# Low halves of the attention weights on GpSimd in quarter pieces, and the RMS root asked earlier

## The reference, cut to what matters

```python
x = x + L0_xattn(layernorm(x), ctx)       # quantized matmul q1 @ q2
x = x + L0_ffn(layernorm(x), ...)         # RMS norm, 24 logits per token, Sinkhorn, mixing
x = x + L1_xattn(layernorm(x), ctx, ...)  # attention with Wq, Wk, biases
x = x + L1_ffn(layernorm(x), ...)         # gated FFN with low-rank terms

# L0_ffn
x_norm = x * rsqrt(mean(x * x) + RMS_EPS)
logits = x_norm @ [W_res; W_pre; W_post].T + base      # 16 + 4 + 4 per token
H_res = sinkhorn_log(H_res_logits)                     # 50 iterations of row and column normalization of a 4x4
H_pre, H_post = softmax(...), softmax(...)
y = (sum_n H_pre[n] * x_n) @ W_branch
out = H_res @ x_streams + H_post[n] * y

# L1_xattn: scores = (text Wq.T + bq)(features Wk.T + bk).T / 32
```

## Time and profile before

| what | value |
|---|---|
| median of 3 runs | 1202.49 us (1200.74 to 1203.63) |
| profiled execution, its own time | 1200.88 us |
| its span, first to last instruction | 1199.1 us |
| TensorE (PE) busy | 1141.1 us, 95% of the span |
| VectorE (DVE) busy | 793.9 us, 66% |
| ScalarE (ACT) busy | 482.3 us, 40% |
| GpSimd (POOL) busy | 149.3 us, 12% |
| mean granted TensorE clock | 0.987 |

### The profile page before, as it was taken

One profiled execution on the slowest core, in us unless ns is written; L12 is line 12 of the kernel. 1 busy time (PEld: TensorE's weight loads), 2 busy tenths in 40 slices (PEclk: granted clock), 3 DMA queues, 4 the chain that ended last, 5 costly groups with the idle time before them and its releaser, 6 DMA issues.

```text
span 1199.1 us, 16583 instructions
## 1 busy us (share of the span) xinstructions
PE 1141.1 (95%) x6452; PEld 569.9 (48%) x6458; DVE 793.9 (66%) x1589; ACT 482.3 (40%) x727; POOL 149.3 (12%) x141
## 2 busy tenths in 40 slices
PE   4877999899989999989999999999999999999998
PEld 2444454644545444554444444444444444444444
DVE  8999889888983278967766767677676552222220
ACT  6785653772253324444434343443433331111110
POOL 4762340081004010200000000000001000000000
PEclk9997999999999999999999999999999999999999
DMA  9620000132032042201121211212112221111310
GB/s 372 250 93 1 2 1 1 71 97 80 1 106 84 7 134 106 106 0 71 36 71 36 71 53 53 71 36 71 36 53 62 98 78 48 48 48 48 131 40 18
DMA packets 26062, 83.58 MB, mean 70 GB/s; under 512 B 3648, under 2 KB 4288, under 8 KB 25984
## 3 DMA queue, kind: packets, MB, share of 16 engines
q1 hardware_dynamic: 25984, 82.53, 19.9%
HBM read 76.22 MB, written 6.29 MB: 69 GB/s over the span
## 4 chain that ended last, share of the span: by engine, by line
PE 72%; DVE 20%; ACT 4%; issue 2%; DMA 1%; POOL 0%; SPq 0%; ACTq 0%; DVEq 0%
PE PAIR L2333 32%; PE PAIR L1975 11%; PE PAIR L1976 11%; PE PAIR L1977 11%; DVE X L1412 2%; DVE PAIR L1364 2%; PE PAIR L2290 1%; DVE LORA L1363 1%; DVE LORA L1365 1%; DVE BST L1214 1%; DVE BST L1215 1%; PE PAIR L2345 1%; DVE X L1285 1%; PE PAIR L2151 1%; DVE XT L1279 1%
## 5 line engine op out<-in xcount | busy, mean ns | idle before, releaser
L1975 PE MATMUL PAIR<-POOL 128*128 128x512 f16 x672 | 255.7, 381 | 2.1 <-DVE POOL L1455 2.1
L1976 PE MATMUL PAIR<-POOL 128*128 128x512 f16 x672 | 255.6, 380 | 0.0
L1977 PE MATMUL PAIR<-POOL 128*128 128x512 f16 x672 | 255.5, 380 | 0.0
L2333 PE MATMUL PAIR<-XT,POOL 128*128 128x512 f16 (+1 forms) x1056 | 239.0, 379 | 1.0 <-ACT ST L889 1.0
L2333 PEld LDWEIGHTS PAIR<-XT,POOL 128*128 128x128 f16 (+1 forms) x1056 | 102.6, 98 | 120.5 <-issue 2.5
L2333 PE MATMUL PAIR<-X,POOL 128*128 128x512 f16 (+1 forms) x528 | 121.2, 379 | 0.0
L1977 PEld LDWEIGHTS PAIR<-POOL 128*128 128x128 f16 x672 | 65.8, 98 | 80.3 <-issue 1.4
L1975 PEld LDWEIGHTS PAIR<-POOL 128*128 128x128 f16 x672 | 65.6, 98 | 67.6 <-DVE POOL L1455 3.9
L1976 PEld LDWEIGHTS PAIR<-POOL 128*128 128x128 f16 x672 | 65.7, 98 | 63.8 <-issue 0.3
L1585 DVE SCALAR_TENSOR_TENSOR STG<-STG,PAIR 128x1024 f32<-128x1024 f32 (+2 forms) x32 | 28.2, 885 | 92.4 <-PE PAIR L2345 89.1
L923 ACT ACTIVATE POOL<-STG 128x1024 f16<-128x1024 f32 (+2 forms) x32 | 25.0, 788 | 145.2 <-DVE STG L1585 145.2
(11 more groups left out here) (296 smaller groups left out, 1738.9 us busy)
## 6 DMA issues: line engine op xcount, KB each, us to landing
STG<-in_gate_w SPq DMA_DIRECT2D x21, 512.0 KB, 3.4
STG<-in_up_w SPq DMA_DIRECT2D x21, 512.0 KB, 4.2
STG<-in_ctx_t SPq DMA_DIRECT2D x16, 512.0 KB, 4.2
STG<-in_ctx SPq DMA_DIRECT2D x16, 512.0 KB, 4.3
STG<-in_down_w SPq DMA_DIRECT2D x16, 512.0 KB, 3.5
POOL<-in_ctx SPq DMA_DIRECT2D x12, 512.0 KB, 11.2
X<-in_x SPq DMA_DIRECT2D x8, 512.0 KB, 9.8
out_t<-X SPq DMA_DIRECT2D x16, 256.0 KB, 2.9
```

Source lines behind the costliest of these rows:

```text
L1975: e.matmul(dst, l_hi, r_hi, start=first, stop=False)
L1976: e.matmul(dst, l_hi, r_lo, start=False, stop=False)
L1977: return e.matmul(dst, l_lo, r_hi, start=False, stop=last)
L2333: i = e.matmul(dst, blk[:, a_, k, :], src[:, b_, k, :], start=(opens and k == 0 and n == 0), stop=(k == KD // 2 - 1 and n == 2), skip_grou ...
```

## The change

GpSimd makes the low halves of weights 0 to 14, each in four instructions of 256 columns instead of one of 1024; VectorE keeps weight 15 alone. ScalarE gives weights 13 and 14 the second pass, and runs `weight_hi(13)` and `weight_hi(14)` directly after `weight_hi(12)`, ahead of `second_transposed(6)`. The RMS root is formed from the variances (`reciprocal(VE)`) instead of from the finished layer-norm scale, so that `logits_root` no longer needs `norm_rest(4, 8)`: VectorE asks for it right after `norm_ask(4, 8)`, and ScalarE takes the two roots one after the other. The part of the logits that needs the means (`logits_mean`) moves up with it, and `bias_operands` moves from between `norm_ask(0, 4)` and `second_lo(4)` to behind it. `second_lo(7)` moves ahead of `norm_rest(4, 8)`.

```diff
-        ON_VECTOR = (13, 14, 15)
+        ON_VECTOR = 15
...
             def weight_lo(i):
                 e.wait_ge(w_hi, i + 1)
-                e.tensor_tensor(W2[i][:, 1, :], FSTAGE[i + AHEAD], W2[i][:, 0, :], ALU.subtract).then_inc(wp_lo, 1)
+                for q in range(0, D, CST):
+                    qs = slice(q, q + CST)
+                    last = e.tensor_tensor(W2[i][:, 1, qs], FSTAGE[i + AHEAD][:, qs], W2[i][:, 0, qs], ALU.subtract)
+                last.then_inc(w_lo, 1)
...
             weight_lo(12)
+            weight_lo(13)
+            weight_lo(14)
             for g in range(NT):
                 branch_sum(g)
...
             weight_hi(12)
+            weight_hi(13)
+            weight_hi(14)
             second_transposed(6)
+            take_logits(0)
             norm_root(4, 8)
-            take_logits(0)
-            weight_hi(13)
+            root(RX2, RX)
             second_transposed(7)
-            weight_hi(14)
             weight_hi(15)
-            root(RX2, RX)
             take_logits(1)
...
             def logits_root():
-                e.wait_ge(ln_ok, 2 * NT)
-                chain(e.tensor_tensor(RN, RST, RST, ALU.mult))
+
+                e.wait_ge(var_ok, 6)
+                chain(e.reciprocal(RN, VE))
                 chain(e.tensor_tensor(RN, RN, MV[:, :, 1], ALU.mult))
                 e.tensor_scalar(RX, RN, RMS_EPS, None, ALU.add).then_inc(var_ok, 1)
+
+            def logits_mean():
+
+                bc = [P, NT, NLOG]
+                e.wait_ge(wsum_ok, 1)
+                chain(e.tensor_tensor(LTMP, MV[:, :, 0].unsqueeze(2).to_broadcast(bc),
+                                      WSUM.unsqueeze(1).to_broadcast(bc), ALU.mult))
...
                 last.then_inc(soft_ok, 1)
-                weight_lo(14)
                 e.wait_ge(sink_a, 2)
...
             norm_ask(0, 4)
-            bias_operands()
             second_lo(4)
             norm_rest(0, 4)
...
             norm_ask(4, 8)
+            logits_root()
+            logits_mean()
+            bias_operands()
             second_lo(6)
+            second_lo(7)
             norm_rest(4, 8)
-            second_lo(7)
-            logits_root()
-            weight_lo(13)
             logits()
```

More of the change, by code:

```diff
@@ L281, in build @@
                              "x_clip", "q_clip"))
-        smh_ok, c2_ok, ht_lo, wp_lo = sem("smh_ok"), sem("c2_ok"), sem("ht_lo"), sem("wp_lo")
+        smh_ok, c2_ok, ht_lo, wv_lo = sem("smh_ok"), sem("c2_ok"), sem("ht_lo"), sem("wv_lo")
         ctx_ok, x1_ok, w_lo, sink_v, soft_v, soft_ok, share_ok, hr_ok, mixed, bias_ok = (
@@ L330, in build @@
             + [(("dfold", m, i), d_add, m * NP + i + 1) for m in range(KD) for i in range(NP)]))
-        ON_VECTOR = (13, 14, 15)
+        ON_VECTOR = 15
         def weight_done(e, i):
-            e.wait_ge(w_lo if i in ON_VECTOR else wp_lo, sum((n in ON_VECTOR) == (i in ON_VECTOR) for n in range(i + 1)))
+            if i < ON_VECTOR:
+                e.wait_ge(w_lo, i + 1)
+            else:
+                e.wait_ge(wv_lo, i - ON_VECTOR + 1)
         def factor_place(n):
@@ L690, in weight_hi @@
                 last = e.activation(W2[i][:, 0, :], st, ACT.Copy, scale=WS)
-                if i not in ON_VECTOR:
+                if i < ON_VECTOR:
                     last = e.activation(st, st, ACT.Copy, scale=WS)
@@ L760, in mix_help @@
                 e.wait_ge(hr_ok, 1)
-                e.wait_ge(wp_lo, 2 * KD - len(ON_VECTOR))
-                e.wait_ge(w_lo, len(ON_VECTOR))
+                weight_done(e, ON_VECTOR - 1)
+                weight_done(e, 2 * KD - 1)
                 for sj in (2, 3):
@@ L1297, in logits @@
                 chain(e.tensor_tensor(RN, RN, RST, ALU.mult))
-                e.wait_ge(wsum_ok, 1)
-                chain(e.tensor_tensor(LTMP, MV[:, :, 0].unsqueeze(2).to_broadcast(bc),
-                                      WSUM.unsqueeze(1).to_broadcast(bc), ALU.mult))
                 e.wait_ge(lg_raw, B)
@@ L1399, in weight_lo @@
                 e.scalar_tensor_tensor(W2[i][:, 1, :], FSTAGE[i + AHEAD], WS, W2[i][:, 0, :], ALU.mult,
-                                       ALU.subtract).then_inc(w_lo, 1)
+                                       ALU.subtract).then_inc(wv_lo, 1)
             def mix(g, sj0=0, sj1=None):
```

## The result

| | before | after |
|---|---|---|
| median | 1202.13 us (1200.74 to 1203.63, 4 runs) | 1195.66 us (1194.12 to 1196.99, 4 runs) |
| profiled execution, its own time | 1200.88 us | 1196.09 us |
| its span | 1199.1 us | 1194.3 us |

The ratio is 0.9941, with a 95% interval of 0.9927 to 0.9956: 7.1 us faster by the ratio, 6.5 by the medians, where 3.8 were forecast. The mechanism came as described in the main: the large links of the chain moved the right way, and two small ones didn't come as forecast (`norm_rest(4, 8)` took turns, and the clock fell again for a shorter time). The gain is nearly twice the sum. So the question for the experiments is which term was too small.

A forecast was written before the change was run, and what follows sets the result against it. TensorE, busy 1141 of 1199 us, was taken as the bound, its waits ended by VectorE's late chain. Chain 2.5 plus clock 1.3 made 3.8 us, from the median 1202.49 to 1198.7; range 1195.2 to 1202.0.

The forecast's parts named there:

- the wait for weight 15: TensorE's wait at M's eighth step, for weight 15's low half: some 2.8 us instead of 4.1.
- The clock: TensorE's granted clock behind M's step 8: 1.3 us taken of the 2.2 us expected if it stays high.
- min(y, x + 2.2): At the mixing: what a gain x on VectorE's chain and y on TensorE's M is worth, in us.
- The log wait: In sinkhorn_start: VectorE must wait for ScalarE's logarithm, so moving out weight 14's 1.13 us saves only 0.5.
- the chain's gain x: VectorE's chain to Sinkhorn gains 2.5 us: 2.1 from its tail and weight 14, 0.4 earlier in the front.
- the last one or two wait a piece: VectorE's norm_rest(0, 4) in GpSimd's gap: small delay at its end, add_product(6) at 84.3 to 84.4, 6.0 us earlier.
- nine instructions that take turns [...] at 0.69 each that is 6.2: Behind norm_ask(4, 8): small VectorE instructions alternate with GpSimd's pieces, 0.69 us each, 6.2 us together.
- this is hidden by 3.4 us: ScalarE's transposed tile 6, held back to 94.3, is still ready before VectorE's second_lo(6) at 97.7.
- `norm_rest(4, 8)` runs free: VectorE's tail to Sinkhorn: GpSimd's lows end at 99.7, so these instructions take no turns and cost 1.2 us.
- the earlier front: Near 41.52 us, small VectorE instructions cross shorter GpSimd pieces: gain between 0 and 0.8 us, 0.4 taken.
- Rival 4: GpSimd's pieces cost 0.53 us each and the clock stays high: 6.5 us gained, 1196.0 us; chance 0.10.
- Rival 3: Pieces cost GpSimd too much: chain gain used up at 0.85 us each, 1205 us at 0.95; chance 0.08.

The follow-up runs named there:

- e7: Changed kernel with weight 15's low half on GpSimd too: 1196.09 us, ratio 0.9949 to the kernel before.
- e11: Changed kernel with bias_operands moved behind the softmax in sinkhorn_start, into the wait for ScalarE's logarithm: 1197.61 us, ratio 0.9955 to the kernel before.
- e1: Kernel before with one edit, GpSimd's low halves in four pieces of 256 columns: 1195.97 us, ratio 0.9957 to the kernel before.
- e3: Changed kernel with bias_operands back between norm_ask(0, 4) and second_lo(4): 1200.04 us, ratio 0.9987 to the kernel before.
- e6: Changed kernel with pieces of 128 columns, eight to a low half: 1206.83 us, ratio 1.0037 to the kernel before.
- e4: Changed kernel with the low halves of weights 13 and 14 back on VectorE: 1196.59 us, ratio 0.9953 to the kernel before.
- e10: e3 with a reciprocal of four numbers put ahead of norm_ask(4, 8): 1200.36 us, ratio 0.9974 to the kernel before.
- e16: e3 with a tensor_tensor of four numbers put ahead of norm_ask(4, 8): one execution, 1201.16 us.
- e17: e3 unchanged, profiled a second time: one execution, 1199.64 us.
- e19: e18 with bias_operands also moved behind the softmax, as in e11: 1197.18 us, ratio 0.9957 to the kernel before.
- e5: Changed kernel with pieces of 512 columns, two to a low half: 1199.58 us, ratio 0.9973 to the kernel before.
- e2: Changed kernel with each GpSimd low half again one instruction of 1024 columns: 1199.75 us, ratio 0.9985 to the kernel before.
- e18: Changed kernel with ScalarE's transposed tiles and roots ahead of the high halves of weights 13 to 15: 1197.67 us, ratio 0.9963 to the kernel before.
- e13: Changed kernel with a reciprocal of four numbers put ahead of norm_ask(4, 8): 1197.46 us, ratio 0.9957 to the kernel before.
- e14: Changed kernel where each piece waits on a semaphore for the piece before it: 1198.80 us, ratio 0.9969 to the kernel before.

## Why the prediction was too small

Right, by its own steps: the wait for weight 15 (forecast 2.8, measured 2.77). The clock (forecast 1.3 us back): from step 8 to the mixing it was 204.56 - 111.40 = 93.16 before and is 197.95 - 105.73 = 92.22, so 0.9 came back. That term was a choice between two outcomes, and neither came whole: the clock fell again, but for 3.6 us instead of 5.8. That 0.9 lies near 1.3 is luck. The rule that ties M and VectorE's chain, min(y, x + 2.2): the chain gained 202.07 - 196.95 = 5.1 (its last instruction, `hr_ok`, starts there), M 6.6, and min(6.6, 7.3) is what the mixing gained. e7 shows the other side: with M far ahead the chain holds the mixing, at 197.79. The log wait was used up as worked out (0.52 us of it left).

The step that failed is one term of the sum, the chain's gain x: "x = 2.5". It measured 5.7 us at weight 15's low half, which starts step 8 (105.73 for 111.40), and 5.1 at the factors; in between one small copy of the Sinkhorn part (L1385, at 138.99) met a GpSimd instruction and took 0.72 us instead of 0.19. So the sum 2.5 + 1.3 = 3.8 came as 5.7 + 0.9 = 6.6 at the mixing. The error of x in its parts:

- **"the last one or two wait a piece"**, `add_product(6)` at 84.3 to 84.4: it came at 81.94. All six instructions passed in GpSimd's gap, since `norm_ask(0, 4)` was issued at 79.57, not 80.51, and took 0.17. Of these 0.94 us, 0.6 were there at 40 us already, 0.5 of them at 11 us, ahead of the first low half; the rest came from the pieces in the front. The 0.5 at 11 us is a difference between two executions (before, VectorE waits 0.56 us for ScalarE there) and not the change's. The 81.94 doesn't hang on it: in the eight profiles with this order, 256 columns and no semaphore wait between pieces, `norm_ask(0, 4)` was issued between 77.64 and 79.88 and `add_product(6)` came between 81.50 and 82.41. 2.4 us, the largest error.
- **"nine instructions that take turns [...] at 0.69 each that is 6.2"**, and 0.2: from 88.83 to 93.26 they took 4.4. Six waited (0.33, 0.60, 0.90, 0.53, 0.59, 0.52), three got in for 0.15 to 0.17, among them two of the three that don't wait for their predecessor (the third is the mean part, L1307, 0.90 us where its own length is 0.36). 2.0 us. A piece is 0.63, not 0.69. The reciprocal that is new in `logits_root` was rightly left out: it needs no turn.
- **"this is hidden by 3.4 us"**, said of ScalarE's transposed tile 6, forecast for 94.3 with VectorE there at 97.7: it was done at 93.16, when VectorE had just arrived (93.13). Had the turns cost nothing, VectorE would have waited here, as e11 shows. `bias_operands`, charged with 3.6, cost nothing.
- **"`norm_rest(4, 8)` runs free"**: it did not. Arriving at 95.57 with pieces until 97.25 it took 2.1 us instead of 1.2, two of its instructions 0.60 each. This error of 0.9 has the other sign.

Together 2.4 + 2.0 - 0.9 = 3.5, nearly the 3.6 us from the forecast 102.5 to VectorE's softmax at 98.90. The 0.4 us that the forecast added for the earlier front is contained in it, which leaves 3.2, the 5.7 less 2.5. e1 shows besides that the moved instructions gave this chain nothing: with the pieces alone it was as early. Rival 4 (cheap pieces, 1196.0) is nearest in time, but not by its mechanism: pieces cost 0.63, not 0.53. The Trainium skill's estimate of 0.56 per piece ("GPSIMD Engine Reference", section "Elementwise — side-by-side cycle accounting") was as far from 0.63 on one side as the row's 0.69 on the other. Its rule of the shared port ("Advanced Engine Details and Errata", section "Mode Summary", where it is stated of VectorE's two-port instructions) held in 195 trains, for `tensor_tensor` too, as a wait for one piece, and the eight long stalls, of up to 24 pieces, go beyond what it says.

Rival 3, slower through GpSimd, was priced for pieces of 0.8 us and more. The danger that the runs showed instead is the standing `norm_ask`: e3 kept 1.6 us of the gain with it, and e6, with two of them and the longer low halves, had a loss. The prediction had no case for it, and the profile of before shows none.

## What to carry to other kernels

Where two engines take turns at a port, the length of one instruction on the slower one is the price of every small instruction on the other; cutting it in four cost that engine 20% more time (2.55 us for 2.13) and gave this kernel 5 us. The reordering around it gave 1 to 2 more at most. Count what really takes a turn (here: not the reciprocals, `bn_aggr` or PSUM readers), place small chains in the other engine's gaps, and look in the profile after for a small instruction that stood over many pieces. When a chain gets faster, look up what was hidden behind it by less than the gain, here ScalarE's transposed tile.

## What the hardware showed that I had not expected

A VectorE instruction of four numbers stood for 3, 6, 6, 7, 8, 11 and 24 boundaries between GpSimd pieces (2.0 to 9.2 us in e4, e3, e10, e16, e17, e6 and e6; 3 again in e19), while its neighbours got in at each boundary. Seven of the eight ended within 0.03 us of the last piece; the longest, e6's second, was let go with four more pieces to come. Alone, with the same instructions, this never came in 195 trains. And the clock's cost behind TensorE's wait for weight 15 came in steps and not with the length of the wait. From step 8 to the mixing it took 90.6 us after waits of 1.3, 1.5, 2.0 and 2.0 us (e17, e10, e16, e3; there to the end of tile 6, as VectorE was later), 92.0 to 92.3 after 2.1, 2.1, 2.3, 2.8, 3.2, 3.4, 3.5 and 6.0 (e6, e5, e2, changed, e4, e11, e18, e19), 93.2 to 93.6 after 3.2, 3.9, 4.1 and 4.1 (e13, e1, e14, before). In e3 the clock is 1.00 from 107 to 117 us, so its 90.6 is the time with nothing lost; against it the others lose about 1.6 us or 2.6 to 3.0.
